# The source of a cast: a fused FFN and attention kernel whose VectorE cast reads the PSUM bank instead of the SBUF copy

## The reference

```python
x = x + 0.5 * ffn(layernorm(x))       # stream f1
x = x + attention(layernorm(x))       # stream at
x = x + 0.5 * ffn(layernorm(x))       # stream f2
# x: [32, 256, 128] float32

# ffn: a mixture of eight experts, four of width 128 and four of width 256
probs = sigmoid(xf @ router_w.T)                # [tokens, 8]
topw, sel = top_k(probs, 2)
topw = topw / (topw.sum(-1) + 1e-20)
combine[t, e] = topw of expert e, or 0
h = square(relu(xf @ W1[e]))
out = sum over e of combine[:, e] * (h @ W2[e])

# attention: 16 heads of 8, rotary embedding, linear
q_feat, k_feat = elu(rope(q) * 8 ** -0.5) + 1, elu(rope(k)) + 1
kv = sum over t of k_feat * v
out = (q_feat @ kv) / max(q_feat . sum(k_feat), 1e-6)
out = out @ W_out
```

## Time and profile before

| | |
|---|---|
| median of three runs | 798.15 us (797.49 to 798.17) |
| the profiled execution | 802.07 us, of it span 800.3 us |
| PE busy | 727.1 us (91%) |
| POOL busy | 686.3 us (86%) |
| ACT busy | 597.6 us (75%) |
| DVE busy | 581.4 us (73%) |
| DMA | 99 GB/s on average |
| mean granted TensorE clock | 0.974 of full speed |

### The profile page before, as it was taken

One profiled execution on the slowest core, in us unless ns is written; L12 is line 12 of the kernel. 1 busy time (PEld: TensorE's weight loads), 2 busy tenths in 40 slices (PEclk: granted clock), 3 DMA queues, 4 the chain that ended last, 5 costly groups with the idle time before them and its releaser, 6 DMA issues.

```text
span 800.3 us, 13031 instructions
## 1 busy us (share of the span) xinstructions
PE 727.1 (91%) x3600; PEld 590.2 (74%) x3600; DVE 581.4 (73%) x1832; ACT 597.6 (75%) x1219; POOL 686.3 (86%) x668
## 2 busy tenths in 40 slices
PE   1788788889999999999999999999999987979977
PEld 1566566667888888888888888888887866767755
DVE  3456688777879798878778786978686768577533
ACT  3577677658888879888888888797878766656755
POOL 3778867869999999999999999999999858666875
PEclk9999999989999999999999999999999989989999
DMA  5553023023323311322333233322223311303230
GB/s 178 185 162 131 19 88 106 1 106 107 106 107 120 106 76 63 128 82 107 119 107 120 107 121 106 120 89 91 69 100 105 120 50 57 120 2 119 119 120 26
DMA packets 31159, 79.36 MB, mean 99 GB/s; under 512 B 3312, under 2 KB 14448, under 8 KB 31088
## 3 DMA queue, kind: packets, MB, share of 16 engines
q1 hardware_dynamic: 30800, 78.47, 28.7%
q10 hardware_dynamic: 288, 0.07, 0.1%
HBM read 73.81 MB, written 4.72 MB: 98 GB/s over the span
## 4 chain that ended last, share of the span: by engine, by line
PE 32%; DVE 28%; POOL 13%; issue 13%; ACT 10%; DMA 3%; DVEq 1%; POOLq 0%; ACTq 0%; SPq 0%
DVE hid L1033 7%; POOL h_lo L866 6%; PE bank L508 4%; PE bank L528 4%; POOL root_f L860 4%; PE bank L529 4%; PE bank L530 4%; PE bank L510 4%; PE bank L509 4%; ACT h_hi L738 2%; DVE pick_f L1011 2%; PE bank L597 2%; DMA g_all_f<-rows_f 2%; PE bank L489 2%; POOL x_lo_at L854 2%
## 5 line engine op out<-in xcount | busy, mean ns | idle before, releaser
L866 POOL TENSOR_TENSOR h_lo<-hid,h_hi 128x512 fp32r<-128x512 f32 x384 | 492.9, 1308 | 77.0 <-ACT h_hi L738 76.4
L1033 DVE SCALAR_TENSOR_TENSOR hid<-bank,g_all_f 128x512 f32<-128x512 f32 x384 | 262.2, 684 | 141.5 <-PE bank L510 101.1
L727 ACT ACTIVATE hid<-hid 128x512 f32<-128x512 f32 x384 | 228.7, 621 | 51.8 <-DVE hid L1033 51.7
L738 ACT ACTIVATE h_hi<-hid 128x512 fp32r<-128x512 f32 x384 | 225.6, 620 | 4.9 <-PE bank L530 0.4
L508 PE MATMUL bank<-x_hi_f,w_hi 128*128 128x512 f32 x384 | 166.4, 433 | 15.2 <-DVE hid L1033 15.1
L528 PE MATMUL bank<-h_hi,w_hi 128*128 128x512 f32 x384 | 157.4, 410 | 10.8 <-POOL h_lo L866 10.8
L510 PE MATMUL bank<-x_hi_f,w_lo 128*128 128x512 f32 x384 | 154.7, 403 | 0.0
L529 PE MATMUL bank<-h_lo,w_hi 128*128 128x512 f32 x384 | 154.3, 402 | 0.0
L530 PE MATMUL bank<-h_hi,w_lo 128*128 128x512 f32 x384 | 153.8, 400 | 0.0
L509 PE MATMUL bank<-x_lo_f,w_hi 128*128 128x512 f32 x384 | 153.7, 400 | 0.0
L508 PEld LDWEIGHTS bank<-x_hi_f,w_hi 128*128 128x128 f32 x384 | 74.1, 193 | 40.4 <-DVE hid L1033 24.5
(11 more groups left out here) (102 smaller groups left out, 1019.1 us busy)
## 6 DMA issues: line engine op xcount, KB each, us to landing
g_all_f<-rows_f SPq DMA_DIRECT2D x128, 512.0 KB, 5.5
x_sb<-in_x SPq DMA_DIRECT2D x16, 256.0 KB, 3.3
out_x<-x_sb SPq DMA_DIRECT2D x16, 256.0 KB, 7.0
g_all_f<-in_w SPq DMA_DIRECT2D x2, 768.0 KB, 6.7
con<-in_const SPq DMA_DIRECT2D x1, 584.0 KB, 6.2
rows_f<-g_row_f SPq DMA_DIRECT2D x32, 16.0 KB, 1.4
g_all_f<-in_wqkv SPq DMA_DIRECT2D x1, 192.0 KB, 6.4
con<-in_const ACTq DMA_DIRECT2D x1, 68.0 KB, 3.1
```

Source lines behind the costliest of these rows:

```text
L727: fn(h, h, ACT.Square).then_inc(s_sq[s], 1)
L738: fn(h_hi[:, c, :], hid[:, c % STAGE, :], ACT.Copy).then_inc(s_hhi[s], 1)
L866: gp.tensor_tensor(h_lo[:, c, :], hid[:, c % STAGE, :], h_hi[:, c, :].bitcast(F32), ALU.subtract).then_inc(s_hlo[s], 1)
L1033: v.scalar_tensor_tensor(hid[:, c % STAGE, :], hp[c % 2][:], 0.0, g_all[s][:, EXPERT[c], :], ALU.max, ALU.mult).then_inc(s_z[s], 1)
```

## The change

VectorE's cast to `x_hi` reads bank 0 instead of `xT`. It waits, as before, for ScalarE's copy of the bank. Since VectorE now reads the bank, the next writer of the bank must wait for the cast: the logits of the same stream and group, and for the attention stream, which has no logits, whatever `tp_free` guards. No instruction is moved, added or removed on any engine; two waits of TensorE are added and one operand changes.

```diff
@@ tp_free @@
                 if due(n[2]):
                     pe.wait_ge(s_xT["at"], value(n[2]))
+                    pe.wait_ge(s_hi["at"], value(n[2]))
@@ logits @@
                 pe.wait_ge(s_xT[s], value(n + 1))
+                pe.wait_ge(s_hi[s], value(n + 1))
@@ high_part @@
                 dve.wait_ge(s_xT[s], value(n + 1))
-                v.tensor_copy(x_hi[s][u][:], xT[s][:]).then_inc(s_hi[s], 1)
+                v.tensor_copy(x_hi[s][u][:], tp[:]).then_inc(s_hi[s], 1)
```

## The result

The changed kernel took 813.85 us (median of 6 runs, 813.29 to 817.47), the kernel before 798.16 on the same chip (median of 6, 795.39 to 800.14). The ratio is 1.0193, 95% interval 1.0167 to 1.022. The forecast of 802.0 with a range of 797.5 to 805.5 was much too low.

A forecast was written before the change was run, and what follows sets the result against it. TensorE was taken to bound the middle, engines in series the start and end. Terms 1.9 + 0.7 + 1.4 + 0.7 - 3.1 + 0 + 2.2 = +3.8 on 802.07 gave 805.9; less 3.92 for the median, 802.0 us, range 797.5 to 805.5.

The forecast's parts named there:

- The middle: 187 to 622 us: GpSimd freed by 0.35 us per iteration, ending PE's ten waits for `hid`: -3.1 us, bounds -3.3 and 0.
- The start: First four groups: logits wait for casts, f1's from the second on behind a `hid` awaiting DMA: +1.9, +0.7, +1.4, +0.7 us.
- the four terms: Delays of groups one to four, with bounds 1.6 to 2.0, 0.3 to 1.4, 0.5 to 2.9 and 0 to 2.0 us.
- 100 to 187 us: Two logits held by 0.15 us, two `root_f` shorter by 0.17: 0 us, bounds -1 and +0.5.
- The end: From 622 us: two f2 transpositions held 0.45 us each, last logits delaying `hid` by 1.3: +2.2 us, bounds 0.9 and 3.
- Slack of the logits: Rival: logits are needed only next iteration, so PE could catch up; sum +0.1, 798.3 us; chance 18%.
- The wait on GpSimd as the real price: Rival: casts skip GpSimd waits, returning 2.2 us more between 100 and 187 us; sum -3.4, 794.8 us; chance 6%.
- TensorE's clock: Rival: PE idling in the start drops to 1.2 GHz; +3, 805 us; sign: fourth group's logits near 2 us; chance 8%.
- Every cast dearer: Rival: each of 48 casts costs VectorE 0.27 us more, no wait changes; +3.6, 801.8 us; chance 3%.

The follow-up runs named there:

- The kernel with both remedies: Changed kernel with f1's cast ahead of the first `hid` up to t = 2 and three 128x110 GpSimd memsets in ten iterations: 798.79 us, ratio 0.9996.
- The waits alone: Changed kernel with the cast reading `xT` on SBUF as before; only TensorE's two new waits stay: 812.01 us, ratio 1.0154.
- after with the larger pad: Changed kernel with three 128x110 memsets on GpSimd ahead of attention's `ve` in each of ten iterations: 810.05 us, ratio 1.0128.
- the kernel before with the early cast: Kernel before the change, with f1's cast ahead of the first `hid` in the first iterations: 797.98 us against 799.27, ratio 0.9977.
- the kernel with `chosen_f` out of the way: Changed kernel with the second `chosen_f` (f2) moved behind the first rotation of k on VectorE: 808.81 us, ratio 1.012.

## Why the prediction was wrong

**What held.** The cast takes 0.68 us in all 48 places and waits for GpSimd nowhere. `root_f` takes 1.63 and three `h_lo` 3.77. `pick_f` ends 0.36 us earlier (0.35 forecast). L489 of the first group, L491 now, starts at 14.54 (14.45 forecast) and the second f1 cast at 28.53 (28.7 forecast). From the start of a cast to the logits held by it lie 0.79 to 0.83 us, where I had 0.72. The sign was right.

**The middle, -3.1 forecast, +7.5 measured.** The step that failed reads "the VectorE work up to the `hid` for which PE waits (L508 at 432.80, 0.29 us idle) moves with it". It did not: between `pick_f` and that `hid` lie 20 us of VectorE's queue, with many `hid` that each need a product of PE first, and the third of them, which waited 0.32 us for PE at 424.53, took the gain back. The kernel with both remedies shows it apart from the collision. The cast is short there, `chosen_f` does not collide, and PE still waits 0.31 us for `hid`: ten waits, 3.5 us in all between 187 and 622, against 3.1 before. So the gain was nothing instead of 3.1; the prediction had itself named PE's waits still being there as a sign of being wrong. The other 7.5 us are the collision, for which the sum had no term at all.

I had used the rule that killed the gain ("`chosen_f`, two operands on SBUF, would then meet the same GpSimd instruction") only for the `chosen_f` next to the cast. The other one, 21 us later, had no wait in the trace of before, so I did not look at how near it was to one. The rows for it were there: it asked within 0.03 us of the start of the third `h_lo`. I forecast that GpSimd would be freed by 0.35 us, which is more than ten times that margin. On this the Trainium skill's page "SBUF — State Buffer", section "Who interferes with whom", says that a VectorE instruction with two SBUF inputs contends with a GpSimd instruction that reads SBUF, and that issue order decides who blocks. The table above agrees, 0.19 to 0.44 us on one side and 1.07 to 1.33 on the other, but for 0.03 us: by the recorded starts a `chosen_f` that came up to 0.025 us behind the `h_lo` still went first.

**The start, +4.7 forecast, +7.2 measured.** The place and the mechanism were right, the sizes not. The first group cost 1.7 (1.9 forecast); the second, third and fourth 1.5, 2.8 and 1.2 (0.7, 1.4 and 0.7 forecast). I had subtracted 1.0, 0.7 and the like for `hid` and statistics that would cover part of the delay. In total almost none of it was covered: I had 1.75, 2.1 and 2.0 us of lateness on TensorE for the three groups, 5.9 in all, and 5.5 arrived at the next casts, each of which stands behind the next `g_all` DMA. Group by group it does not fit as well (the third's 2.8 is more than my 2.1, the fourth's 1.2 less than my 2.0). The upper bounds of the four terms add up to 8.3 and would have held; my range did not carry them. The waits alone cost 7.8 us at 104 (after 7.2) and 9.8 at 187 (after 5.7). Of the difference that opens behind 104, 1.9 us lie between 104 and 170. There the casts of the waits-alone kernel still sit out GpSimd instructions, and PE now waits for them: the f1 casts at 111.92 and 143.44 take 1.50 and 1.13 us, and the logits behind them wait 0.94 and 0.57 us, where after has 0.68 and 0.67 us for the casts and two waits of 0.11. The other 1.6 us are those of the next paragraph.

**100 to 187 us, 0 forecast, -1.5 measured** by the casts at 104.13 and 187.29 in before. Of this -1.6 lies in the last 17 us, from the cast at 170.49. The windows of before and of after for it (length; busy PE, PEld, DVE, ACT, POOL; clock, DMA, GB/s):

```profile
170.49:187.29 16.80, 15.43 (x72) 12.85 (x73) 12.12 (x47) 12.80 (x30) 10.69 (x12) 0.90 0.06 19
```

```profile
177.81:192.99 15.18, 13.81 (x72) 11.30 (x73) 12.11 (x47) 12.78 (x30) 10.69 (x12) 1.00 0.08 21
```

The work is the same, 72 products of PE, and takes 1.62 us less of PE, as much as the stretch is shorter; the granted clock is 1.00 instead of 0.90. In before it is at 1.2 GHz from 171.2 to 174.6 us. The other kernels' traces say the same: the six with full clock in this stretch gain 1.61 to 1.63 us on before, and the seven others, which like before have some 3 us of it at 1.2 GHz, gain 0 to 0.5. So these 1.6 us belong to TensorE's clock, not to the cast. Why the clock falls in some of the traces there was not isolated.

**The end, +2.2 forecast, -1.3 by the two traces.** The held products are there:

```profile
671.82 0.41 PE L471 MATMUL bank<-con,xn_f 128*128 128x128 f32 x2 [0.64 <-DVE x_hi_at L953]
...
765.40 0.77 PE L491 MATMUL bank<-router_sb,xT 128*128 128x96 f32 x5 [0.82 <-DVE x_hi_f L953]
```

These two rows are of the timeline of after; the view ends inside both groups of products. But from 622 us to the end single executions differ by more than such a term: -1.3 in after, +1.9 in after with the larger pad, -2.3 in the kernel before with the early cast. The granted clock is a part of this. In before's trace it is at 1.2 GHz for 24.9 us of this stretch and PE is busy for 152.69 us, in after's for 18.1 and 150.83, with 711 products each. By an estimate from these numbers 1.9 us of after's gain are the clock's, and +0.6 would be left for the held products. The size of this term stays open. The 3.8 us by which the medians differ more than the two traces have at least this in them: before's profiled execution is one with a low clock (0.974; after's has 0.983). Of 29 executions of before on one chip, those with a mean clock up to 0.976 took 800.6 us in the mean and those from 0.982 on 797.9.

**The rivals.** Slack of the logits: no. The wait on GpSimd as the real price: no, though the casts did lose their waits. TensorE's clock: not as the cause of the loss. Where it is recorded, from 24 us in before and 26 us in after up to the fifth f cast, each of the two has 10.2 us at 1.2 GHz, and over the span after's clock is the higher one (0.983 against 0.974). In after the fourth group's logits took 1.10 us (81.93), not near 2. But the second group's took 1.82 instead of 1.16, and in the kernel with `chosen_f` out of the way, whose program is that of after up to there, the third and the fourth group's took 2.00 and 1.99 and the fifth f cast came 1.6 us later than in after. So the clock does scatter single executions by this much. Nor does it fall each time PE has stood idle: in after it falls at 29.5 and 56.8 us, with the held logits of the second group and behind those of the third, but not behind those of the fourth, before which PE was idle for 2.59 us. Every cast dearer: no, VectorE's time for casts fell from 41.3 to 32.8 us. None of them was the collision elsewhere, which was worth 7.5 of the 11.9 us between the traces.

## What to carry over

A saving on an engine that is off the critical path shifts the phase of all its later instructions against those it excludes. Before forecasting a gain, look in the steady iteration for every instruction that may share the resource, not just for those that wait now, and read how far each is from the start of the other engine's next one: a margin smaller than the shift is the term to price, here at up to a whole GpSimd instruction per iteration, and at nothing where no wait of the bounding engine stands behind it. And if a gain has to travel through a queue, name the next wait in it that is ended by the engine you want to relieve, because the gain stops there.

Where a second reader holds a bank, a product of TensorE inherits everything that stands in front of that reader in its own queue, a DMA wait included; the order in that queue is then the thing to change, and doing so here brought the fifth f cast from 7.2 us late to within 1.7 us of before's. And before a difference between two single traces is put down to a change, compare the granted clock of the same stretch in both: here it was worth 1.6 us in 17.

## What the hardware showed beside this

- A VectorE instruction of about 0.15 us with two operands on SBUF takes 1.07 to 1.35 us if it asks 0.028 to 0.32 us behind the recorded start of a GpSimd instruction of 1.3 us. If it asks at the start or up to 0.025 us behind it, it takes 0.18 to 0.20, and the GpSimd instruction takes up to 1.38. A change of 0.03 us in its start changed the iteration by 1.1 us (43.57 to 44.69).
- Memsets of 128x8 on GpSimd last 0.10 to 0.11 us each in the profile, but three of them in a row moved what follows by only 0.10 us in all; three of 128x110, of 0.18 to 0.23 us each, moved it by 0.40.
- The kernel runs no faster with a cast that takes 0.68 us for certain than with one of 0.41 to 1.53: 798.79 against 799.27 us (95% interval of the ratio 0.9981 to 1.0012), and against 797.98 us with the same early cast and the old source, once order and phase are as before.
